# The last 32 channels turned side by side in a fused Swin-block kernel (one transpose for up to four tiles), second high copy of the attention outputs by ScalarE

## The reference, cut to what matters

```
x3 = concat(depthwise 9x9 conv of relu(x) into 144 channels, relu(x))     # 8 images, 56 x 56 tokens, DIM = 160
for shift, mask in ((0, None), (3, MASK1)):            # two Swin blocks, windows of 7 x 7, 5 heads of 32
    z  = layernorm(x3); q, k, v = split(window_partition(roll(z)) @ qkvw + qkvb)
    o  = softmax(q @ k.T * 32**-0.5 + bias + mask) @ v
    x1 = x3 + window_reverse(o @ projw + projb)
    x3 = x1 + gelu(layernorm(x1) @ w1 + b1) @ w2 + b2
y = x3 @ linw + linb, then a 9x9 synthesis conv and a 1x1 conv
```

## Time and profile before

| | |
|---|---|
| median of 3 runs | 2950.16 us (2948.86 to 2952.37) |
| the profiled execution | 2952.52 us, span from first to last instruction 2951.0 us |
| mean granted clock of PE | 0.986 of full speed |
| PE busy | 2883.9 us, 98% |
| DVE busy | 2213.6 us, 75% |
| ACT busy | 1721.5 us, 58% |
| POOL busy | 837.1 us, 28% |

### The profile page before, as it was taken

One profiled execution on the slowest core, in us unless ns is written; L12 is line 12 of the kernel. 1 busy time (PEld: TensorE's weight loads), 2 busy tenths in 40 slices (PEclk: granted clock), 3 DMA queues, 4 the chain that ended last, 5 costly groups with the idle time before them and its releaser, 6 DMA issues. The chain is left out here.

```text
span 2951.0 us, 94022 instructions
## 1 busy us (share of the span) xinstructions
PE 2883.9 (98%) x39898; PEld 2703.9 (92%) x39898; DVE 2213.6 (75%) x6736; ACT 1721.5 (58%) x4076; POOL 837.1 (28%) x1470
## 2 busy tenths in 40 slices
PE   8979999999999999999999999999999999999799
PEld 6669999999999999999999999999999999999799
DVE  5667777887787777787788878778878878887422
ACT  6446666666666666666656655565656555665321
POOL 8122222222222222222323322232323332332111
PEclk9969999999999999999999999999999999999899
DMA  6321111111111111111112221121111111112374
GB/s 155 128 90 25 40 46 43 46 43 46 43 43 30 42 43 46 43 46 43 46 26 47 58 58 34 33 44 44 42 24 44 44 44 25 42 43 46 65 136 77
DMA packets 210768, 152.23 MB, mean 52 GB/s; under 512 B 15954, under 2 KB 205205, under 8 KB 210331
## 3 DMA queue, kind: packets, MB, share of 16 engines
q1 hardware_dynamic: 207619, 142.41, 21.0%
q10 hardware_dynamic: 1008, 3.44, 0.5%
q0 software_dynamic: 1728, 0.48, 0.2%
HBM read 95.64 MB, written 52.50 MB: 50 GB/s over the span
## 5 line engine op out<-in xcount | busy, mean ns | idle before, releaser
L1627 PE MATMUL rm<-w,ht 128*112 128x160 f32 x4480 | 676.5, 300 | 0.0
L1627 PEld LDWEIGHTS rm<-w,ht 128*112 128x112 f32 x4480 | 619.7, 177 | 11.8
L1051 POOL TENSOR_TENSOR rs<-ln_tmp,mhalf 112x4 f32<-112x4 f32 (+1 forms) x128 | 118.8, 928 | 980.3 <-DVE ln_tmp L1233 980.3
L1148 ACT ACTIVATE ht<-rm 128x336 f32<-128x336 f32 (+1 forms) x448 | 216.6, 490 | 124.6 <-PE rm L147 124.5
L1091 ACT ACTIVATE qm<-ra,qpair 128x400 f32<-128x400 f32 x256 | 138.1, 590 | 214.4 <-PE ra L147 214.4
L1124 ACT ACTIVATE pt<-pt_ps 113x490 f32<-113x490 f32 x256 | 149.4, 584 | 184.7 <-PE pt_ps L1566 184.7
L1005 POOL TENSOR_TENSOR z<-z,one 112x448 f32<-112x448 f32 (+2 forms) x192 | 131.4, 684 | 358.2 <-DVE z L1237 358.2
L1119 ACT ACTIVATE pr<-sm 113x490 f32<-113x490 f32 x256 | 159.5, 623 | 88.4 <-DVE sm L1296 87.7
L1338 DVE TENSOR_TENSOR ot_lo<-ra,ot_hi 128x98 fp32r<-128x98 f32 x512 | 109.1, 255 | 128.1 <-ACT ot_rest L1131 118.0
L1131 ACT ACTIVATE ot_hi<-ra 128x98 fp32r<-128x98 f32 x512 | 102.1, 259 | 141.3 <-PE ra L1601 141.3
L1296 DVE TENSOR_TENSOR sm<-sc,mx 113x490 f32<-113x490 f32 x256 | 177.6, 694 | 6.6
(11 more groups left out here) (276 smaller groups left out, 9231.8 us busy)
## 6 DMA issues: line engine op xcount, KB each, us to landing
xa<-xs SPq DMA_DIRECT2D x128, 245.0 KB
xr<-xs SPq DMA_DIRECT2D x128, 245.0 KB
xs<-xo SPq DMA_DIRECT2D x64, 245.0 KB
ys<-yz SPq DMA_DIRECT2D x64, 245.0 KB
c_y<-ys SPq DMA_DIRECT2D x36, 260.0 KB
xs<-a_tok SPq DMA_DIRECT2D x14, 560.0 KB, 6.1
xs<-tok_late SPq DMA_DIRECT2D x14, 560.0 KB, 6.7
a_nat<-in_x ACTq DMA_DIRECT2D x7, 480.0 KB, 6.2
```

Source lines behind the costliest of these rows:

```text
L1148: act_(ht[:, f * SN + t0 * TT:f * SN + (t0 + nt) * TT], bank_m(i, lm, use)[:, 0:nt * TT], ACT.Gelu_apprx_tanh).then_inc(m_freed(i, lm, use ...
L1627: last = mm(bank_m(i, lm, use)[0:TT, t * DIM:(t + 1) * DIM], ht[:, c:c + TT], keep.w["w2", lm][:, f * DIM:(f + 1) * DIM], start=(f == 0), ...
```

## The change

The last 32 channels of up to four tiles are turned by one transpose: they are put side by side first (POOL's `rest_apart` into new tiles `z1r` and `z2r`, 32 columns for each tile; DVE's `outputs` into columns 256 to 319 of `os_`), one transpose gives a PSUM bank with tile `t` in rows `32 t` to `32 t + 31`, and ACT and DVE take each tile from its own rows. The three parts of the rest tile are made behind the turn: ACT writes the high part with one instruction for each tile, DVE the low part with one for each tile, and the second high part is written, for `z1` and `z2`, by a DVE copy within SBUF (rows 0 to 31 to rows 64 to 95), and for the outputs by two more ACT instructions from the PSUM bank. PE waits for the rest tile only ahead of the fourth pass (`rest_ready`), does the first three passes of Q and K ahead of their fourth ones, and does `weights_turned(2)` behind `mlp_out(1)` instead of ahead of it.

```diff
-def split_passes(nc, out, hi, lo, rest, w_hi, w_lo, w_rest, act_moves):
+def split_passes(nc, out, hi, lo, rest, w_hi, w_lo, w_rest, act_moves, rest_ready=None, passes=range(4)):
-    for n, (a, w) in enumerate(pairs):
+    for n in passes:
+        a, w = pairs[n]
+        if n == 3 and rest_ready is not None:
+            nc.tensor.wait_ge(*rest_ready)
...
-                once = view(t, 0, TT, t0 * ZW + 128, [[ZW, nt], [0, 2], [1, REST]])
-                gp.tensor_tensor(view(t, 0, TT, t0 * ZW + DIM, [[ZW, nt], [REST, 2], [1, REST]]), once,
-                                 view(one, 0, TT, 0, [[0, nt], [0, 2], [0, REST]]), ALU.mult).then_inc(s, 1)
+            def rest_apart(t, r, s, t0=0, nt=ST):
+                gp.tensor_tensor(view(r, 0, TT, t0 * REST, [[REST, nt], [1, REST]]),
+                                 view(t, 0, TT, t0 * DIM + 128, [[DIM, nt], [1, REST]]),
+                                 view(one, 0, TT, 0, [[0, nt], [0, REST]]), ALU.mult).then_inc(s, 1)
...
+                    act.wait_ge(*a_full(i, f"T1C{hf}"))
+                    for t in range(nt):
+                        last = act_(view(z1t[2], 0, REST, (t0 + t) * WIN, [[WP, 16], [1, WIN]]),
+                                    view(bank_a(i, f"T1C{hf}"), t * REST, REST, 0, [[WIN, 16], [1, WIN]]), ACT.Copy)
+                    last.then_inc(s_hi1, 1)
...
-                    for dst, rows, c0 in ((ot[0], 128, 0), (ot[2], CR, 2 * QP)):
+                    for p in range(2):
+                        act_(view(ot[0], 0, 128, (2 * j + p) * WIN, dims),
+                             view(bank_a(n, use), 0, 128, p * QP, [[WP, 2], [WIN, WIN], [1, WIN]]), ACT.Copy)
+                    for p0 in (0, 2 * REST):
                         for p in range(2):
-                            last = act_(view(dst, 0, rows, (2 * j + p) * WIN, [[W, 2], [TT, WIN], [1, WIN]]),
-                                        view(bank_a(n, use), 0, rows, c0 + p * QP, [[WP, 2], [WIN, WIN], [1, WIN]]), ACT.Copy)
+                            last = act_(view(ot[2], p0, REST, (2 * j + p) * WIN, dims),
+                                        view(bank_a(n, use), p * REST, REST, 2 * QP, [[WP, 2], [WIN, WIN], [1, WIN]]), ACT.Copy)
...
+                    for t in range(nt):
+                        ins = v.tensor_tensor(view(z1t[2], REST, REST, (t0 + t) * WIN, dims),
+                                              view(bank_a(i, f"T1C{hf}"), t * REST, REST, 0, [[WIN, 16], [1, WIN]]),
+                                              view(z1t[2], 0, REST, (t0 + t) * WIN, dims).bitcast(F32), ALU.subtract)
+                    ins.then_inc(a_freed(i, f"T1C{hf}")[0], 1)
+                    dims = [[WP, 16], [1, nt * WIN]]
+                    v.tensor_copy(view(z1t[2], 2 * REST, REST, t0 * WIN, dims),
+                                  view(z1t[2], 0, REST, t0 * WIN, dims).bitcast(F32)).then_inc(s_rest1, 1)
...
-                    v.tensor_tensor(view(os_, 0, QP, 128, [[ZW, 2], [HD, 3], [1, HD]]),
-                                    view(so, 0, QP, OC + 4 * VW, [[512, 2], [0, 3], [1, HD]]),
-                                    view(rd, 0, QP, 4, [[HEADS, 2], [0, 3], [0, HD]]), ALU.mult).then_inc(s_od, 1)
+                    v.tensor_tensor(view(os_, 0, QP, 256, [[REST, 2], [1, HD]]),
+                                    view(so, 0, QP, OC + 4 * VW, [[512, 2], [1, HD]]),
+                                    view(rd, 0, QP, 4, [[HEADS, 2], [0, HD]]), ALU.mult).then_inc(s_od, 1)
...
+                    ins.then_inc(s_lo3, 1)
+                    for p in range(2):
+                        o = (2 * j + p) * WIN
+                        ins = v.tensor_tensor(view(ot[2], REST, REST, o, dims),
+                                              view(bank_a(n, use), p * REST, REST, 2 * QP, [[WP, 2], [WIN, WIN], [1, WIN]]),
+                                              view(ot[2], 0, REST, o, dims).bitcast(F32), ALU.subtract)
...
-                    for t in range(nt):
-                        c = (t0 + t) * ZW + f0
-                        last = tr(bank_of(use)[0:rows, t * TT:(t + 1) * TT], z[:, c:c + rows], keep.ident[0:TT, 0:TT])
+                    if part == "A":
+                        for t in range(nt):
+                            c = (t0 + t) * DIM
+                            last = tr(bank_of(use)[:, t * TT:(t + 1) * TT], z[:, c:c + 128], keep.ident[0:TT, 0:TT])
+                    else:
+                        last = tr(bank_of(use)[0:nt * REST, 0:TT], zr[:, t0 * REST:(t0 + nt) * REST],
+                                  keep.ident[0:TT, 0:TT])
...
-                if la is not None:
-                    weights_turned(2, i)
                 if lm is None and la is None:
                     pe.wait_ge(s_clear, 2)
                 if lm is not None:
                     mlp_out(1)
+                if la is not None:
+                    weights_turned(2, i)
                 if ln is not None:
-                    front_product("Q", 0)
-                    front_product("K", 0)
+                    front_product("Q", 0, range(3))
+                    front_product("K", 0, range(3))
+                    front_product("Q", 0, range(3, 4))
+                    front_product("K", 0, range(3, 4))
                     front_product("B", 0)
...
-                    pe.wait_ge(*a_freed(i, "OT3"))
+                    pe.wait_ge(s_lo3, NG * (i + 1))
                     projection(0)
```

More of the change, by code:

```diff
@@ L1034, in front_rest @@
                     pool.wait_ge(s_norm[0], n + 1)
-                    repeat_rest(z1, s_z[0])
+                    rest_apart(z1, z1r, s_z[0])
                 if lm is None and la is None:
@@ L1080, in front_hi @@
                     t0, nt = HALF[hf]
[L1081 to L1085, removed]
+                    act.wait_ge(*a_full(i, f"T1A{hf}"))
+                    act_(view(z1t[0], 0, 128, t0 * WIN, [[WIN, nt], [WP, 16], [1, WIN]]),
+                         view(bank_a(i, f"T1A{hf}"), 0, 128, 0, [[TT, nt], [WIN, 16], [1, WIN]]), ACT.Copy).then_inc(s_hi1, 1)
+                    act.wait_ge(*a_full(i, f"T1C{hf}"))
[3 more added lines that the diff above has]
+                    last.then_inc(s_hi1, 1)
                 def queries(hf):
@@ L1136, in t_hi @@
                     t0, nt = HALF[hf]
[L1137 to L1141, removed]
+                    act.wait_ge(*turned_full(i, lm, f"T2A{hf}"))
+                    act_(z2t[0][:, t0 * TT:(t0 + nt) * TT], turned_bank(i, lm, f"T2A{hf}")[:, 0:nt * TT],
+                         ACT.Copy).then_inc(s_hi2, 1)
+                    act.wait_ge(*turned_full(i, lm, f"T2C{hf}"))
+                    for t in range(nt):
+                        last = act_(z2t[2][0:REST, (t0 + t) * TT:(t0 + t + 1) * TT],
+                                    turned_bank(i, lm, f"T2C{hf}")[t * REST:(t + 1) * REST, 0:TT], ACT.Copy)
+                    last.then_inc(s_hi2, 1)
                 def gelu(g):
@@ L1345, in t_lo @@
                     cols = slice(t0 * TT, (t0 + nt) * TT)
[L1346 to L1351, removed]
+                    dve.wait_ge(s_hi2, hi2(m, 2 * hf + 1))
+                    v.tensor_tensor(z2t[1][:, cols], turned_bank(i, lm, f"T2A{hf}")[:, 0:nt * TT], z2t[0][:, cols].bitcast(F32),
+                                    ALU.subtract).then_inc(turned_freed(i, lm, f"T2A{hf}")[0], 1)
+                    dve.wait_ge(s_hi2, hi2(m, 2 * hf + 2))
+                    for t in range(nt):
+                        one = slice((t0 + t) * TT, (t0 + t + 1) * TT)
+                        ins = v.tensor_tensor(z2t[2][REST:2 * REST, one],
+                                              turned_bank(i, lm, f"T2C{hf}")[t * REST:(t + 1) * REST, 0:TT],
+                                              z2t[2][0:REST, one].bitcast(F32), ALU.subtract)
+                    ins.then_inc(turned_freed(i, lm, f"T2C{hf}")[0], 1)
+                    v.tensor_copy(z2t[2][2 * REST:CR, cols], z2t[2][0:REST, cols].bitcast(F32)).then_inc(s_rest2, 1)
                 def mlp_out(n):
@@ L1476, in _, with turn @@
             mm, tr = nc.tensor.matmul, nc.tensor.transpose
-            def turn(z, hf, bank_of, room, full, name, freed_already=()):
+            def turn(z, zr, hf, bank_of, room, full, name, freed_already=()):
                 t0, nt = HALF[hf]
-                for part, f0, rows in (("A", 0, 128), ("C", 128, CR)):
+                for part in "AC":
                     use = f"{name}{part}{hf}"
@@ L1598, in outputs_turned @@
                         reach(pe, *a_room(n, use))
[L1599 to L1602, removed]
+                    for p in range(2):
+                        tr(bank_a(n, use)[:, p * QP:(p + 1) * QP], os_[:, p * 128:(p + 1) * 128], keep.ident[0:QP, 0:QP])
+                    last = tr(bank_a(n, use)[0:2 * REST, 2 * QP:3 * QP], os_[:, 256:256 + 2 * REST],
+                              keep.ident[0:QP, 0:QP])
                     last.then_inc(a_full(n, use)[0], 1)
```

74 lines of the change are left out of this document (41 added, 33 removed).

## The result

The changed kernel takes 3014.92 us (median of four runs, 3010.38 to 3015.89), the kernel before 2949.51 us beside it. The ratio is 1.0217 (95% interval 1.0201 to 1.0233): 65 us slower, where 3050 was forecast with a range of 2970 to 3095. The profiled execution has a span of 3014.2 us, before 2951.0.

A forecast was written before the change was run, and what follows sets the result against it. PE's list plus its waits was taken to bound the kernel; -0.27 + 0.93 + 0.64 + 0.34 = +1.64 us a body, over 62 bodies 102 us on 2950, gave 3050 us, range 2970 to 3095.

The forecast's parts named there:

- What bounds the kernel: Whole body: PE is busy 98%, so its list plus its waits set the time; ACT's and DVE's delivery times matter.
- What PE is spared: PE's list: 14 transposes fewer a body at 0.10 us each, 1.4 us a body, 87 us were all else hidden.
- The price of a held instruction: Small ACT and DVE instructions with changing start rows run at full duration: 0.30 us on ACT, 0.295 on DVE, 112 columns.
- The head: From mlp_turned(0) to the start of front_turned(0): saved transposes outweigh waits of 0.15 and 0.18 us, -0.27 us a body.
- T to S: From front_turned(0)'s start to the first score of scores(0): longer ACT and DVE work delays Q, +0.93 us a body.
- S to O: From the first score of scores(0) to outputs_turned(3): longer outputs_hi(2) and outputs_lo(2) delay os, +0.64 us a body.
- O to the projection: From outputs_turned(3) to the projection's fourth pass: longer ACT and DVE copies make it later, +0.34 us a body.
- (a): Rival on ACT's and DVE's small copies: nothing is held, they overlap; -0.95 us a body, 2891 us, chance 0.12.
- (b): Rival on the small copies: only DVE is held, ACT overlaps; about -0.6 us a body, 2912 us, chance 0.04.
- (c): Rival on the small copies: only ACT is held, the head's two waits go; +0.8 us a body, 3000 us, chance 0.08.
- (d): DVE's copy within SBUF: as forecast but at full price, +1.95 us a body, 3070 us; chance 0.74 together with the forecast.
- The signs: Trace: ACT copies 0.30 us apart, outputs_hi 1.4 us, z1t_hi back to back, PE idle some 3 us a body, busy less.

The follow-up runs named there:

- The experiment on its start rows: Changed kernel with ACT's small copies on unchanged start rows in the first half's part C and outputs_hi(1) alone: 2983.23 us, ratio 1.0113 against the kernel before.
- The edit of group 2 alone: Changed kernel with ACT's small copies on unchanged start rows in outputs_hi(2) alone: 2989.99 us, ratio 1.0138 against the kernel before.

## Why the prediction was right, point by point

*What bounds the kernel.* Right: PE's list, and how early ACT and DVE deliver. ACT's busy share rose from 58% to 66%, yet the start rows of its copies alone were worth 95 us.

*What PE is spared.* Right: 896 transposes at 0.10 us. With both engines' start rows unchanged 63 us of the 87 came through; PE's new order, which cost 7 us alone, is in that kernel too.

*The price of a held instruction.* Right in kind, somewhat high in size: 0.265 us on ACT for 112 columns (forecast 0.30) and 0.28 on DVE (0.295); `outputs_hi` 1.32 us (1.38). My 0.28 us for one ACT copy came from `ot_rest` over 96 rows; the ones over 32 rows, also of 98 columns, have a mean of 0.247 us (four of them in 1.02 us in the row of `outputs_hi` above). The copies within SBUF were 0.06 us shorter than forecast: 448 columns 0.39 us, `z1`'s 336 columns 0.33 (forecast 0.45 and 0.39, from scalings with a scalar operand). `z2`'s copy of 336 columns is the exception, 0.40 us on the mean and 0.47 in this body; no run tells why.

```profile
2058.13 0.39 DVE L1384 CAST z2t_rest<-z2t_rest 32x448 fp32r<-32x448 f32 x1
```

*The head.* The term that was off most: -0.27 forecast, -0.62 measured in the second block. Its two stalls of 0.15 and 0.18 did not come there. The first was a sum of nine small durations, taken a little too long: ACT's copies end at 2056.94 and the DVE copy at 2058.52, 3.65 us behind the start of the body where I had 3.95, and the fourth pass starts at 2058.66, 3.79 behind it, on time. In the first block, which I had taken to be like the second, part of the second stall did come: `outputs_turned(0)` waits for `os`, 0.32 us on the weight load, and starts 0.10 us later in the body than in the second block. The head is -0.44 there.

```profile
1028.65 0.20 PEld L1641 LDWEIGHTS ra<-ident,os 113*128 113x128 f32 x2 [0.32 <-DVE os L1336]
```

*T to S.* +0.66 for +0.93: the same two chains, each held copy 0.02 to 0.04 cheaper and the DVE copy 0.06. Q's first pass stands at T+6.50 (forecast 6.65, before 6.20), its fourth at T+7.86 (8.17, before 6.89), and the scores follow ACT's `k`, which ends at 2080.99, by 0.14 us. The experiment on its start rows shows the chain: its copies on unchanged rows give back 0.58.

*S to O and O to the projection.* +0.53 and +0.29 for +0.64 and +0.34. The projection's first pass was not quite hidden (it starts at O+2.37, before at O+2.26, and its weight load waits 0.27 us for `ot_lo`), but the fourth pass behind it waits once more, for `ot_rest`, and sets the time. The edit of group 2 alone, forecast at -0.4 a body, gave 25 us and moved S to O only.

*The rivals.* (a), nothing held, 2891 us: the kernel with unchanged rows on both engines ran in 2887. (b), only DVE held, 2912: the one with ACT's rows unchanged ran in 2920. (c), only ACT held, 3000: 2979. The last one is not quite case (c), for only the input's rows were made equal on DVE. The mechanisms are told apart, and the changed kernel is none of them. (d), the copy at full price, fell by the 0.39 us of the copy.

*The signs.* ACT's copies, `outputs_hi` and the back-to-back `z1t_hi` came as written. "Some 3 us" of idle time a body was too much: the loads of weights are idle for 151 us more than before, 2.4 a body, and the matmul rows for 70, 1.1 a body. PE's busy time fell by 7 us and that of the weight loads by 88, where "up to 87" stood. Why the matmul rows show so little of both is not worked out.

*The sum.* 62 x 1.64 = 102 us was forecast, 65 measured. The mechanism and its three places were right, and all four terms were too high. Of the 0.78 us a body that were too much in the second block, 0.35 are the head, 0.27 T to S, 0.11 S to O and 0.05 the projection; in the first block the sum is 0.60, with 0.17 for the head. Both are above the error of 0.3 us a body that the prediction allowed itself, and 3015 as the lower end with such an error does not follow from its numbers (3050 less 20 is 3030). The result is at the edge of that inner range, and well inside the stated one, which had been drawn down to 2970 to take in case (c).

## What to carry to other kernels

Count, for an edit that saves TensorE instructions, what it does to the delivery times behind it and not to the busy shares: here some 63 us of PE's savings were there to have, and the consumers' start rows cost 128 (3015 against 2887). Cutting one copy over 96 rows into several that each start at another group of 32 rows cost their full durations in series here; on the same rows they were half as far apart on ScalarE and two thirds on VectorE. Take such a change part by part: the one at a place with slack (z2, -1.0%) is worth having, the same edit on a tight chain is not.

## What the runs showed of the hardware

In these runs ScalarE holds an instruction back until the one ahead has ended when the start row of its PSUM input changes, as VectorE does. Copies of 112 columns over 32 rows are 0.265 us apart when they read bank rows 0, 32, 64, 96, and one lasts 0.259; they are 0.14 us apart when all read from row 0, and one lasts 0.248. The means of one copy, in the changed kernel and with both engines' rows unchanged:

```profile
L1092 ACT ACTIVATE z1t_rest<-ra 32x112 fp32r<-32x112 f32 x448 | 116.1, 259 | 5.1 <-PE ra L1522 1.4
```

```profile
L1093 ACT ACTIVATE z1t_rest<-ra 32x112 fp32r<-32x112 f32 x448 | 77.1, 248 | 2.5 <-PE ra L1524 2.5
```

VectorE's subtractions are 0.28 us apart when held and 0.18 when not, and one lasts 0.270 or 0.257. The Trainium skill ("VectorE: DVE Perf Modes", section "Two Vector instructions with no wait between them") states the hold for VectorE, for a change of the input's or of the output's start quadrant. The runs agree where only the input's row changes; a change of the output's row alone was not tried on either engine. For ScalarE these runs are the evidence.
